# A two-layer graph network kernel on one core: where the steps of the general path stand, and when a dense stage's x rows are loaded

## The reference

```python
def _sage_conv(x, src, dst, W_l, b_l, W_r):
    agg = segment_sum(x[src], dst, 12500)
    deg = segment_sum(ones, dst, 12500)
    return agg / maximum(deg, 1)[:, None] @ W_l + b_l + x @ W_r
h = relu(_sage_conv(x, src, dst, W1_l, b1, W1_r))
h = relu(_sage_conv(h, src, dst, W2_l, b2, W2_r))
out = layernorm(x + h @ W3 + b3)
```

## Time and profile before

| what | us |
|---|---|
| median of 3 runs (lowest, highest) | 3479.47 (3472.67, 3479.57) |
| the profiled execution's own time | 3487.17 |
| its span, first to last instruction | 3485.4 |
| GpSimd busy (x2455) | 2414.8, 69% |
| TensorE busy | 2821.9, 81% |
| VectorE busy | 1467.9, 42% |
| mean granted TensorE clock | 0.928 of full |

### The profile page before, as it was taken

One profiled execution on the slowest core, in us unless ns is written; L12 is line 12 of the kernel. 1 busy time (PEld: TensorE's weight loads), 2 busy tenths in 40 slices (PEclk: granted clock), 3 DMA queues, 4 the chain that ended last, 5 costly groups with the idle time before them and its releaser, 6 DMA issues.

```text
span 3485.4 us, 62735 instructions
## 1 busy us (share of the span) xinstructions
PE 2821.9 (81%) x13209; PEld 2327.4 (67%) x13210; DVE 1467.9 (42%) x3299; ACT 483.7 (14%) x1411; POOL 2414.8 (69%) x2455
## 2 busy tenths in 40 slices
PE   4878898798788799798666778888878889888856
PEld 2555677677577577687554657777767777777745
DVE  7665455455455454433332333333333333333333
ACT  2001101001101111111100111121111111111112
POOL 2667676576677577677665777777777777777765
PEclk7899999999999999999888899999999999999988
DMA  3344776676576577576654446766757757757664
GB/s 83 106 138 131 222 219 191 184 239 208 172 228 210 161 227 237 179 228 207 190 175 121 123 122 195 214 196 195 224 168 213 223 174 221 216 175 223 208 198 147
DMA packets 496439, 652.87 MB, mean 187 GB/s; under 512 B 184189, under 2 KB 414579, under 8 KB 493140
## 3 DMA queue, kind: packets, MB, share of 16 engines
q0 software_dynamic: 117504, 321.02, 31.2%
q1 hardware_dynamic: 298036, 254.07, 23.6%
q10 hardware_dynamic: 80800, 76.82, 7.2%
HBM read 581.29 MB, written 70.40 MB: 187 GB/s over the span
## 4 chain that ended last, share of the span: by engine, by line
PE 26%; POOL 23%; issue 17%; DVEq 13%; DMA 10%; DVE 7%; PEld 2%; ACT 1%; PEldq 1%; SPq 1%; ACTq 0%; POOLq 0%
POOL ring L405 23%; PE ps L486 14%; PE ps L557 5%; DMA ring<-z_rows,scol 3%; DVEq L888 2%; PE psY L601 2%; DMA scratch<-in_x 2%; DMA work<-in_x 2%; DVE oh L942 1%; DVEq L908 1%; DVE oh L900 1%; PE psY L590 1%; PEld ps L486 1%; DVE acc L878 1%; DMA scratch<-z_rows 1%
## 5 line engine op out<-in xcount | busy, mean ns | idle before, releaser
L486 PE MATMUL ps<-ring,oh 128*125 128x257 f32 (+1 forms) x6416 | 1621.8, 405 | 404.8 <-DMA ring<-z_rows,scol 184.6
L486 PEld LDWEIGHTS ps<-ring,oh 128*125 128x125 f32 x6416 | 1250.2, 200 | 692.6 <-issue 493.5
L405 POOL DMA_INDIRECT ring<-in_x,scol x1224 | 1208.4, 987 | 621.0 <-issue 346.1
L405 POOL DMA_INDIRECT ring<-z_rows,scol x1224 | 1205.8, 985 | 425.7 <-issue 358.9
L900 DVE SCALAR_TENSOR_TENSOR oh<-dcol,cf,iota 128x500 f32<-128x500 int16 x802 | 593.8, 740 | 987.2 <-PE ps L486 749.8
L557 PE MATMUL ps<-scratch 128*125 128x257 f32 (+1 forms) x2000 | 491.9, 394 | 44.0 <-DMA scratch<-in_x 29.7
L557 PEld LDWEIGHTS ps<-scratch 128*125 128x125 f32 x2000 | 460.4, 295 | 70.5 <-DMA scratch<-in_x 32.1
L878 DVE TENSOR_TENSOR acc<-ps,acc x806 | 339.4, 421 | 290.0 <-issue 238.1
L531 PE MATMUL psB<-oh 128*128 (+1 forms) x540 | 164.4, 400 | 98.4 <-DVE oh L942 96.4
L1200 ACT COPY work<-psY 125x256 f32<-125x256 f32 x100 | 37.3, 373 | 1381.1 <-PE psY L590 1381.1
L1235 ACT ACTIVATE work<-psT 128x250 f32<-128x250 f32 x100 | 37.7, 377 | 1229.1 <-PE psT L652 1229.0
(11 more groups left out here) (119 smaller groups left out, 1140.3 us busy)
## 6 DMA issues: line engine op xcount, KB each, us to landing
scratch<-counts SPq DMA_DIRECT2D x200, 312.5 KB
scratch<-in_x SPq DMA_DIRECT2D x114, 512.0 KB, 4.2
scratch<-z_rows SPq DMA_DIRECT2D x114, 512.0 KB, 4.4
counts<-scratch SPq DMA_DIRECT2D x25, 1250.0 KB
work<-in_x ACTq DMA_DIRECT2D x200, 125.0 KB
ring<-in_x,scol POOLq DMA_INDIRECT x1224
ring<-z_rows,scol POOLq DMA_INDIRECT x1224
scratch<-in_x SPq DMA_DIRECT2D x114, 128.0 KB, 4.5
```

Source lines behind the costliest of these rows:

```text
L405: pool.indirect_dma_start(ring[:, slot, b, 0:D], None, rows_dram, bass.IndirectOffsetOnAxis(scol[:, n - C0:n - C0 + 1], 0)).then_inc(rows[ ...
L486: mm = pe.matmul(psA[0:WN, bass.ds(bank, W)], oh[:, 2 * (slot % 2) + later, b, :], ring[:, slot, b, 0:W], start=(b == 0), stop=(b == nb - 1))
```

## The change

It moves the 20 fallback steps of each layer. At the end of layer one each of the last 20 groups of the loop is followed by one step (and the inner loop is gone: the four steps stand in the loop's body). In layer two the steps leave the end and stand in the first 40 groups, one after each second group; `fallback_start` goes ahead of them. SyncE's loads of `z_rows` for these steps come first in layer two. Besides, in layer one the rows `x` of a stage's first two steps are loaded before the wait on `s_kept`, their counts behind it.

```diff
-            def load_step(rows_dram, w, t):
+            def load_counts(w, t):
                 q = t % 2
-                place(q)
                 sp.dma_start(lin_a[:, q].rearrange("p f n j -> p f (n j)"),
...
-                load_rows(rows_dram, t, s_lin[q])
+
+            def load_step(rows_dram, w, t):
+                place(t % 2)
+                load_counts(w, t)
+                load_rows(rows_dram, t, s_lin[t % 2])
...
             for w in range(HW):
+                for t in range(2):
+                    place(t)
+                    load_rows(x, t, s_lin[t])
                 sp.wait_ge(s_kept, credit[s_kept] + 16 * PARTS * (w + 1))
-                for t in range(STEPS):
+                for t in range(2):
+                    load_counts(w, t)
+                for t in range(2, STEPS):
                     load_step(x, w, t)
...
+            fallback(z_dram)
             for w in range(HW):
                 for t in range(STEPS):
                     load_step(z_dram, w, t)
-            fallback(z_dram)
...
-                def four(builds=False, dense=False, general=False):
+                def four(builds=False, dense=False, general=()):
...
+                        if i in general:
+                            fallback(l, general.index(i) % 2)
...
                     with pe.Fori(0, STEPS // 2):
-                        four()
+                        four(general=(1, 3))
...
                 with pe.Fori(0, STEPS // 4):
-                    four()
-                    with pe.Fori(0, 2):
-                        fallback(l, 0)
-                        fallback(l, 1)
+                    four(general=(0, 1, 2, 3) if l == 0 else ())
```

More of the change, by code:

```diff
@@ L1090, in finish, with four @@
                         v.reg_mov(fin, until)
-                def four(builds=False, w=None):
+                def four(builds=False, w=None, general=()):
                     for i in range(4):
@@ L1099, in four @@
                             finish(row_of(i)[3])
+                        if i in general:
+                            fallback(l)
                     if w is not None:
@@ L1121, in layer @@
                             four(w=w)
+                    fallback_start()
                 else:
+                    fallback_start()
                     with v.Fori(0, STEPS // 2):
-                        four()
+                        four(general=(1, 3))
                     with v.Fori(0, HW) as w:
@@ L1129, in layer @@
                             four(w=w)
-                fallback_start()
                 with v.Fori(0, STEPS // 4):
[L1132 to L1135, removed]
+                    four(general=(0, 1, 2, 3) if l == 0 else ())
                 for i in range(TAIL_GROUPS):
```

## The result

The changed kernel takes 3450.28 us (3443.77 to 3452.8, 4 runs) beside 3476.07 us of the kernel before: a ratio of 0.9923 (95% interval 0.9903 to 0.9943). That is 27 us by the ratio, 26 by the medians. Timed again later beside the kernel before (e13), it was 0.9916 (0.9901 to 0.9931), 29 us by the ratio and 28 by the medians. I had forecast 55 us and a range that ended at 3448. The direction was right, half of the gain is missing. The profiled execution took 3452.8 us, 34 us less than the one of before.

A forecast was written before the change was run, and what follows sets the result against it. GpSimd's gather pace was taken as the bound, with only its waits for TensorE to gain. The terms 25.5 + 20 + 10 = 55.5 us, with 0 for layer two's start, took the median from 3479.5 to 3424 us, range 3409 to 3448.

The forecast's parts named there:

- What bounds the kernel: Whole kernel: GpSimd's own gather pace is the bound; an edit gains only from its 311.7 us of waits for TensorE.
- Part 1: End of layer one, one step after each group: loads asked for two groups ahead end TensorE's pauses; gain 25.5 us.
- a rival with a chance of 0.10: End of layer one: VectorE reloads code at four jumps back of a 388-instruction loop; total 3434 us, chance 0.10.
- Part 2: End of layer two, no steps left there: the pauses go altogether; gain 20 us, bounds 17 and 21.3.
- Part 3: First forty groups of layer two, one step after each second group: cost 0, bounds 0 and 5 us.
- the slower rival: Layer two's start: step loads delay the gathers and TensorE becomes the bound; total 3499 us, chance 0.03.
- Part 4: Layer one's stage starts, x rows loaded ahead of the counts' landing: gain 10 us, bounds 2 and 20.
- Crowded DMA engines: End of layer one: loads at share 0.76 land too late, half of the gain there stays; 3437 us, chance 0.10.
- That the move does nothing: Moved fallback steps: waits only go elsewhere, leaving the early x rows' gain alone; total 3470 us, chance 0.03.
- Layer two's gathers: Sign to look for at the start of layer two: its gathers start about 35 us earlier (25.5 + 10).

The follow-up runs named there:

- e13: The changed kernel itself, unaltered, timed again beside the kernel before on a 3475 us chip: 3447.2 us, 0.9916 of the kernel before.
- e17: The kernel before with only the x rows of a stage's first two steps loaded ahead of the counts' wait: 1.0009 of the kernel before.
- e15: The changed kernel with VectorE's general-step halves rolled into a loop and the first x rows loaded before the last counts' store: 3419.5 us, 0.9826 of before.
- e2: The changed kernel with two general steps after each second group, on VectorE an inner loop, 262 instructions long: 0.9905 of the kernel before.
- e4: The kernel before with VectorE's inner loop of fallback steps written out at the end of both layers: 1.0074 of the kernel before.
- e9: The changed kernel itself, unaltered, on a chip where the kernel before took 4203 us: 0.9967 of the kernel before.
- e10: The changed kernel with VectorE's general-step halves rolled into a loop and the x rows back behind the counts' wait, same slow chip: 0.9952 of before.

## Why the prediction was wrong, point by point

**What bounds the kernel** held. GpSimd's waits for TensorE fell by 36 us and the profiled execution by 34.

**Part 1, end of layer one: forecast 25.5 us.** Measured from the first gather of group 280 to the last of the layer: 162.2 us before, 143.2 after and 144.3 in e13, so 18 to 19 us. With the reload undone it is 132.1 to 136.9 us: 25 to 30 us, the forecast or more. The mechanism for TensorE's loads was right, those asked for two groups ahead land in time. The step that failed is "What is late next is TensorE waiting now and then for a load": the sum had 3 us for that and nothing for VectorE, whose jump back it left to a rival with a chance of 0.10. What was late next was VectorE's one-hot matrix, 25.7 us of TensorE's waits against 4.2 for loads, and it cost 10 us of the stretch. The rival was right in its mechanism, its sign and its size (I took 10 us), though it priced the jumps back alone and not the pauses within the loop. I had the rows for it: a pause of 2.94 and 2.33 us in a loop of 404 instructions, no such pause in VectorE's timeline of the loop of 260, and 388 in the change. The reason I gave against it, the place in the list, was no observation. By the traces, loops of 262 and 308 instructions run free, those of 388 to 391 and 404 pause at every jump back. The rule that I cited (the Trainium skill, Runtime: NRT & Kernel Launch, Instruction fetch mechanics: two pages of 256 instructions, a branch out of them fetches) pointed the same way, and the traces agree with it: packets of instructions arrive in the pauses. Where the pages begin no row shows. A small misreading besides: TensorE's five pauses at the end of layer one were 7.9 to 12.3 us long, those of layer two 8.1 to 10.5, not 9 to 12.

**Part 2, end of layer two: forecast 20 us.** 155.9 us before, 136.9 after, 136.2 in e13: 19 to 20 us. Right in mechanism; the size leans on one profile, for e17, whose layer two is that of the kernel before, had 150.9.

**Part 3, first forty groups of layer two: forecast 0.** 208.5 us before, 204.6 after, 203.8 to 207.2 in all kernels of the 3475 us chips that have the steps there; GpSimd's waits for TensorE in it come to 0.3 to 2.5 us. Right, and the slower rival, contention there, did not come.

**Part 4, rows ahead of the counts' landing: forecast 10 us of gain, bounds 2 and 20.** The five waits grew by 6 us and the time by 3 (e17, not clear of noise), with 8 to 10 in one comparison. This is the larger error, 13 us or so. The step that failed is "the two steps' rows stand ahead of it in the same queue, so I take 3.8": the rows, 1.25 MB, were put between the store and the count load, and I named them but priced the load below the 4.3 us median of a load alone, as if they had left. It took 5.3. I also let the lower bound stop at a gain, although the sentence for it ("the rows delay the counts as much as they are out of the way") describes a wait that is only moved; nothing excluded a loss. I did not price the store itself at all: it lands 1.2 us later. The same idea works where the rows have a free stretch, as e15 shows: 12 us less of waits than with the rows late.

**The other rivals.** Crowded DMA engines: the share rose to 0.70 and TensorE had one wait of 4.2 us for rows; e2, with burstier loads and shorter waits, speaks against it as a cause. That the move does nothing: no. Layer two's gathers start 20 us earlier, where the forecast had 35: the 10 of part 4 and some 6 of part 1 are what is missing.

The sum by what the runs showed is 18.5 + 19.5 - 3 (part 4, e17) = 35 us. The two profiled executions differ by 34, but that agreement is in part luck. By stretches, the ends of the layers are 19.0 and 19.0 us shorter, the first forty groups of layer two 3.9 and layer one up to group 280 0.7 shorter, and groups 40 to 280 of layer two 9.4 us longer, which is scatter. The timed runs differ by 27 and 29 us by their ratios: the profiled execution of before, 3487.2 us, was slower than each of the four timed ones (3472.6 to 3479.6). The 6 to 8 us between 35 and these are put down to no stage by any run; part 2's 5 us between two profiles of the same code show how easily they arise.

## What to carry to other kernels

Before code is written out in a loop, count the loop's instructions on each engine: where an engine's trace shows pauses behind the jump of its longest loop, expect them in any other loop that grows near that length, even if the code it gains never runs. The instruction queue's packets in that stretch tell whether they came. And a transfer that is moved ahead of a wait is only out of the way if the queue it is moved to is idle then; ask what stands behind it, and put it where nothing does.

## What the runs showed of the hardware that I had not expected

VectorE's pauses are not only at the jump back (3.8 to 6.4 us in the changed kernel) but also at forward jumps over code that isn't run, 1.4 to 3.4 us, three times in the changed kernel and in every pass of e4. The profile page's row of the instruction queue counts them: 81 packets without, 102 with, 123 with both layers.

The same program took 3447 us on one chip and 4190 on another (e13, e9). VectorE's instructions last as long (the addition of L885 0.42 us in both). TensorE's clock was granted at 0.869 there and at 0.937 here, and it was busy 3048.5 and 2816.0 us. That is 232 us of TensorE, less than the 734 between the two spans; the rest is waits between engines: GpSimd's for TensorE grew from 278.3 to 807.4 us, TensorE's for VectorE from 94.1 to 412.3. What causes them wasn't tried, nor whether the lower clock is a cause or follows from the waits. An edit's worth may be half or nothing on such a chip, as e9 and e10 show.
